# The down product of a mixture of experts turned: weights stationary, tokens moving

## What is computed

```python
gate = softmax(x @ Wg + bg); thr = sigmoid(x @ Wt + bt) * 0.125
adapted = gate - thr; w = adapted * (adapted >= 0)
w = w / where(sum(w) == 0, 1, sum(w))
h = gelu(einsum('td,edf->etf', x, W1) + b1[:, None, :])
eo = einsum('etf,efd->etd', h, W2) + b2[:, None, :]
out = einsum('te,etd->td', w, eo)
x = x + gb * out
```

## Time and profile before

| | |
|---|---|
| median of 3 runs | 1946.36 us (1943.92 to 1947.73) |
| the profiled execution, its own time | 1949.09 us |
| span of its trace | 1947.3 us |
| PE busy | 1807.6 us, 93%, 11616 matmuls |
| weight loads (PEld) | 1627.2 us, 84% |
| DVE, ACT, POOL busy | 1304.9 us (67%), 1048.1 us (54%), 756.0 us (39%) |
| DMA | 56.04 MB, 56434 packets |

### The profile page before, as it was taken

How to read it: one execution, slowest core, us unless ns; L and a number is a source line. 1 busy time by engine, 2 the same in 40 slices (tenths; PEclk the granted TensorE clock), 3 DMA queues, 4 the chain that set the end, 5 groups by cost and what they waited for, 6 DMA issues and landing times.

```text
span 1947.3 us, 32671 instructions
## 1 busy us (share of the span) xinstructions
PE 1807.6 (93%) x11616; PEld 1627.2 (84%) x11616; DVE 1304.9 (67%) x2472; ACT 1048.1 (54%) x2072; POOL 756.0 (39%) x1163
## 2 busy tenths in 40 slices
PE   5789947899589999999999999999999999999997
PEld 4679845798578999999999998888999999999996
DVE  3778747787666666666666666768666666666666
ACT  2567634676454555555555555554555555555553
POOL 4332124333364351615335161739244260624403
PEclk7999968999899999999999999999999999999998
DMA  4000000000000100101010010112110010101002
GB/s 112 26 15 23 18 11 17 23 18 9 31 23 23 33 23 22 42 4 44 11 34 31 14 44 1 33 33 89 53 33 22 23 34 12 44 12 33 12 1 65
DMA packets 56434, 56.04 MB, mean 29 GB/s; under 512 B 8384, under 2 KB 54480, under 8 KB 56272
## 3 DMA queue, kind: packets, MB, share of 16 engines
q1 hardware_dynamic: 56272, 53.95, 9.1%
HBM read 45.55 MB, written 8.39 MB: 28 GB/s over the span
## 4 chain that ended last, share of the span: by engine, by line
PE 62%; issue 5%; DVE 2%; ACT 2%; POOL 1%; POOLq 0%; DVEq 0%; ACTq 0%
PE score_ps L1075 10%; PE score_ps L1076 10%; PE score_ps L1077 9%; PE tr_ps L1110 5%; PE tr_ps L1108 5%; PE tr_ps L1106 5%; PE m_ps L1110 3%; PE m_ps L1108 3%; PE m_ps L1106 3%; PE o_ps L1108 3%; PE o_ps L1110 3%; PE o_ps L1106 3%; DVE h_lo L1276 1%; ACT h_hi L1209 1%; POOL h2f L1437 0%
## 5 line engine op out<-in xcount | busy, mean ns | idle before, releaser
L1205 ACT ACTIVATE g_sb<-c_sb,b_cols 128x512 f32<-128x512 f32 x384 | 276.0, 719 | 439.3 <-DVE c_sb L1340 288.1
L1276 DVE TENSOR_TENSOR h_lo<-g_sb,h_hi 128x512 fp32r<-128x512 f32 x512 | 398.6, 800 | 105.0 <-ACT h_hi L1209 105.0
L1075 PE MATMUL score_ps<-t_hi,w_hi 128*128 128x512 f32 x896 | 361.3, 403 | 27.6 <-ACT p_u L1235 12.2
L1076 PE MATMUL score_ps<-t_lo,w_hi 128*128 128x512 f32 x896 | 355.8, 397 | 0.0
L1077 PE MATMUL score_ps<-t_hi,w_lo 128*128 128x512 f32 x896 | 350.8, 392 | 0.0
L326 POOL TENSOR_TENSOR w_sums<-w_raw 128x128 f32<-128x128 f32 x64 | 42.7, 667 | 664.1 <-PE m_ps L1110 663.3
L1108 PE MATMUL tr_ps<-w_both,h_hi 128*128 128x256 f32 x1024 | 290.6, 284 | 0.0
L1110 PE MATMUL tr_ps<-w_both,h_lo 128*128 128x256 f32 x1024 | 290.5, 284 | 0.0
L1106 PE MATMUL tr_ps<-w_both,h_hi 128*128 128x256 f32 x1024 | 289.3, 283 | 0.0
L1209 ACT ACTIVATE h_hi<-c_sb,b_cols 128x512 fp32r<-128x512 f32 x384 | 271.6, 707 | 0.0
L1075 PEld LDWEIGHTS score_ps<-t_hi,w_hi 128*128 128x128 f32 x896 | 170.9, 191 | 54.5 <-ACT p_u L1235 12.2
(11 more groups left out here) (191 smaller groups left out, 4377.5 us busy)
## 6 DMA issues: line engine op xcount, KB each, us to landing
w_raw<-w_dram SPq DMA_DIRECT2D x128, 256.0 KB, 3.2
x_sb<-x_dram SPq DMA_DIRECT2D x32, 128.0 KB, 2.3
x_scratch<-x_sb SPq DMA_DIRECT2D x32, 128.0 KB, 1.7
t_sums<-x_scratch SPq DMA_DIRECT2D x8, 512.0 KB, 4.6
out_dram<-h2f SPq DMA_DIRECT2D x7, 512.0 KB, 3.2
probs_even<-wmod_dram SPq DMA_DIRECT2D x4, 256.0 KB, 3.9
probs_even<-wmod_dram SPq DMA_DIRECT2D x4, 128.0 KB, 2.3
probs_odd<-wqkvT_dram SPq DMA_DIRECT2D x1, 512.0 KB, 5.8
```

Source lines behind the costliest of these rows:

```text
L1075: nc.tensor.matmul(bank, hi, t_hi[p][:, b_, :], start=start, stop=False, skip_group_check=True)
L1076: nc.tensor.matmul(bank, hi, t_lo[p][:, b_, :], start=False, stop=False, skip_group_check=True)
L1205: nc.scalar.activation(g_sb[:, m % 2, :], source, ACT.Gelu_apprx_tanh, bias=bias).then_inc(act_g, 1)
L1276: nc.vector.tensor_tensor(h_lo[:, m % 6, :], g_sb[:, m % 2, :], h_hi[:, m % 6, :].bitcast(F32), ALU.subtract).then_inc(dve_lo, 1)
```

## The change

The down product is turned: the stationary operand is a block of 128 hidden by 128 model columns of W2, high or low part, and all 512 tokens of a unit of hidden values move. Its result is [model columns, tokens], one bank for each of two blocks of model columns and each unit. So the gate of a token now lies along the free dimension and has to be the same on all partitions: the gates are written to DRAM transposed, element by element, on SP at the end of each batch of attention, and a row of 1024 tokens is loaded for each round to all partitions (g_rows). b2 lies on partitions and is added in the eviction. The eviction is one DVE instruction per bank, `(y + b2) * g`, four per round; for expert 0 it writes the accumulator, for the others y_sb, which POOL adds to the accumulator. At the end the accumulator is transposed back by PE through bank_b (16 turns, each in a group of its own: 72 to 79 and 121 to 128, and four more at the very end), scaled by the output gate on DVE and added to x1 on POOL. The bias product is gone. Weight slots go from five to four, the hidden ring from six to five. The casts of the next pair's tokens move on ACT from the end of a group to behind p_u; the low parts of the token sums go from POOL to DVE.

```diff
-SLOTS = 5
+SLOTS = 4
+RING = 5
...
+gT_dram = nc.dram_tensor("gates_scratch", [B, E, T], F32).ap()
...
+                    for half in range(NT // GT):
+                        sp.wait_ge(*done(dve_G2, b, "G2", half, 0, G2_STEPS))
+                        for t in range(half * GT, (half + 1) * GT):
+                            sp.dma_start(gT_dram[b, :, t * P:(t + 1) * P].rearrange("e p -> p e"),
+                                         gates[:, b * NT + t, :], allow_slow_non_contiguous=True).then_inc(s_gT[b], 16)
...
+                    sp.dma_start(b2_cols[:], b2.rearrange("e (k p) -> p e k", p=P), allow_slow_non_contiguous=True).then_inc(l_b2, 16)
...
+                    def load_gates(r):
+                        b, e, p = parts(r * FS)[0:3]
+                        if e == 0 and p == 0:
+                            sp.wait_ge(s_gT[b], NT * 16)
+                        if r > 0:
+                            sp.wait_ge(dve_evict, r * 4)
+                        sp.dma_start(g_rows[:], gT_dram[b, e, p * 2 * UTOK:(p + 1) * 2 * UTOK].partition_broadcast(
+                            P)).then_inc(l_g, 16)
...
 def down(n, name):
-                        for j in range(UNIT):
-                            tok = slice(j * P, (j + 1) * P)
-                            nc.tensor.matmul(y_of(u, j), h_hi[:, ring, tok], w2_both[slot][:, f, 0, :], ...)
-                            nc.tensor.matmul(y_of(u, j), h_hi[:, ring, tok], w2_both[slot][:, f, 1, :], ...)
-                            nc.tensor.matmul(y_of(u, j), h_lo[:, ring, tok], w2_both[slot][:, f, 0, :], ...)
+                        for k in range(KD):
+                            if first and before >= 0:
+                                pe.wait_ge(dve_evict, before * 4 + u * 2 + k + 1)
+                            w_hi, w_lo = (w2_both[slot][:, f, i, k * P:(k + 1) * P] for i in range(2))
+                            o = y_banks[u][k]
+                            nc.tensor.matmul(o, w_hi, h_hi[:, ring, :], ...)
+                            nc.tensor.matmul(o, w_lo, h_hi[:, ring, :], ...)
+                            nc.tensor.matmul(o, w_hi, h_lo[:, ring, :], ...)
...
 def evict(n, u):      (DVE, in place of add)
+                        dve.wait_ge(l_g, (r + 1) * 16)
+                        to = acc_of(b, p, u) if e == 0 else y_sb[:, u, :, :]
+                        for k in range(KD):
+                            nc.vector.scalar_tensor_tensor(to[:, k, :], y_banks[u][k], b2_cols[:, e, k:k + 1],
+                                                           g_rows[:, u * UTOK:(u + 1) * UTOK], ALU.add,
+                                                           ALU.mult).then_inc(dve_evict, 1)
...
 def add(r):           (POOL)
+                        for u in range(2):
+                            pool.wait_ge(dve_evict, r * 4 + u * 2 + 2)
+                            nc.gpsimd.tensor_tensor(acc, acc, y_sb[:, u, :, :], ALU.add).then_inc(pool_acc, 1)
...
 def turned(...):      (PE)
+                        for i, t in enumerate(tiles):
+                            for k in range(KD):
+                                last = nc.tensor.transpose(bank[:, i * D + k * P:i * D + (k + 1) * P],
+                                                           source[:, k, t * P:(t + 1) * P], ident_sb[:])
+                        last.then_inc(made_by, 1)
...
 ACT loop
                         nc.scalar.activation(p1_u3[:], bank_a, ACT.Copy).then_inc(act_p1, 1)
+                        cast_tokens(n)
                         act.wait_ge(pe_prod, 7 * n + 3)
                         hidden(n, "c11", bank_a)
...
 DVE, before its loop
+                    dve.wait_ge(l_b2, 16)
```

More of the change, by code:

```diff
@@ new lines, in down, with turned, turn @@
+                        done_.then_inc(pe_down, 1)
+                    def turned(source, bank, tiles, made_by):
+                        for i, t in enumerate(tiles):
[3 more added lines that the diff above has]
+                        last.then_inc(made_by, 1)
+                    def turn(n):
+                        k = TURN_AT[n]
+                        b, p, u, half, r = turn_source(k)
+                        pe.wait_ge(dve_u2, min(n + 1, GROUPS))
+                        pe.wait_ge(pool_acc, adds_before(r, u) + 1)
+                        turned(acc_of(b, p, u), bank_b, (2 * half, 2 * half + 1), pe_turn)
@@ L1183, in _ @@
                             product(n, bank_h, S4, B22, False, True)
+                        else:
+                            pe.wait_ge(dve_evict, LAST * 4 + 2)
+                            for i, bank in enumerate((bank_a, bank_g)):
+                                if i == 0:
+                                    pe.wait_ge(act_hi, made(GROUPS - 1, "c11") + 1)
+                                else:
+                                    pe.wait_ge(dve_c21, GROUPS)
+                                turned(y_sb[:, 0, :, :], bank, (2 * i, 2 * i + 1), pe_fin)
                         if n > 0:
                             down(n - 1, "c12")
+                    pe.wait_ge(dve_evict, LAST * 4 + 4)
+                    pe.wait_ge(dve_c12, GROUPS)
+                    turned(y_sb[:, 1, :, :], bank_h, (0, 1), pe_fin)
+                    pe.wait_ge(dve_turn, len(TURNS))
+                    turned(y_sb[:, 1, :, :], bank_b, (2, 3), pe_fin)
                 @block.scalar
@@ L1248, in _ @@
                         hidden(n, "c12", c_sb[:, 0, :])
-                        cast_tokens(n)
                 @block.vector
@@ L1376, in _ @@
-                    nc.vector.tensor_tensor(half, half, slabs[1][:, 0:2, :], ALU.add).then_inc(dve_out, 1)
+                    turn(GROUPS)
+                    dve.wait_ge(dve_c22, GROUPS)
+                    dve.wait_ge(dve_c12, GROUPS)
+                    for i, (to, bank) in enumerate(((p1_u3[:], bank_a), (u2[:], bank_g))):
+                        dve.wait_ge(pe_fin, i + 1)
+                        scaled(to, bank, B - 1, dve_fin)
+                    evict(GROUPS - 1, 1)
+                    dve.wait_ge(dve_lo, 4 * GROUPS)
@@ new lines, in _ @@
+                    for i, (to, bank) in enumerate(((g_sb[:, 0, :], bank_h), (g_sb[:, 1, :], bank_b))):
+                        dve.wait_ge(pe_fin, i + 3)
+                        scaled(to, bank, B - 1, dve_fin)
+                    dve.wait_ge(dve_fin, 4)
+                    dve.wait_ge(pool_out, len(TURNS))
+                    tile = slabs[3].rearrange("p t d -> p (t d)")[:, 2 * D:4 * D]
+                    nc.vector.tensor_tensor(tile, tile, g_sb[:, 1, :], ALU.add).then_inc(dve_out, 1)
```

348 lines of the change are left out of this document (163 added, 185 removed).

## The result

The changed kernel takes 2068.5 us (median of 4 runs, 2060.0 to 2079.2), the kernel before 1947.1 beside it: ratio 1.063, 95% interval 1.058 to 1.068. The range ended at 1980. The profiled execution took 2060.0 us.

A forecast was written before the change was run, and what follows sets the result against it. TensorE's order of matmuls was taken to set the mixture's time. Terms -21 - 17 - 12 - 8 + 15 + 35 + 8 - 2 gave -2 us, 1944 from the median 1946.4, range 1918 to 1980.

The forecast's parts named there:

- Gate rows through DRAM: 32 element-wise gate DMAs on SP: batch 0's hide, batch 1's delay the mixture's start; +8 us, bounds +2 and +41.
- Down product: 48 matmuls of 256 columns become 24 of 512 per group: -21 us, bounds 0 and -23.
- Bias, token preparation: Bias work leaves expert 0's 16 groups, -17 us; token casts, sums and low parts move to waiting places, -12.
- Old finish, turning back: POOL's old work finishing both batches goes, -8 us; twenty turns of four transposes each come, +15, bounds +9 and +20.
- Sums on GpSimd: Two 1024-element POOL additions in 27 rounds hold up DVE's h_lo: +35 us, bounds 25 to 51, from below about 5.
- Tail: Work behind the last matmul gets some 2 us shorter: -2 us, bounds -4 and +1.
- Rival C: Element-wise DMA delays the mixture's start; at 3.2 us per gate DMA +34, 1978 us; chance 0.13.
- Rival E: The turned down product saves little or nothing, something else sets the step: +13 to +21, 1957 to 1965 us; chance 0.07.
- the walk: One round followed with a 2.4 us POOL addition behind each half's eviction: 1.3 us lost per round, 27 rounds, +35.
- Rival B: POOL's additions cost little, 0.3 us a round, 8 instead of 35, gate rows 3: 1912 to 1930 us; chance 0.26.
- D: Rival: the port is worse, additions at 2.8 us, two stalls, 2.5 us per round: +32, 1976 us; chance 0.12.

The follow-up runs named there:

- e1: The kernel before plus only the 32 gate DMAs in 4-byte pieces to DRAM, which nothing reads: 2100.7 us, ratio 1.080 to the kernel before.
- e5: e3 with each GpSimd sum cut to 16 elements per partition, leaving most expert results out of the output: 1871.3 us, ratio 0.959 to the kernel before.
- e3: The changed kernel with gates and b2 turned on TensorE instead of moved element by element: 1905.7 us, ratio 0.979 to the kernel before.
- e9: The kernel before plus only batch 0's sixteen gate DMAs in 4-byte pieces, which nothing reads: 2005.6 us, ratio 1.029 to the kernel before.
- e2: The changed kernel with gates turned on TensorE, b2 still loaded element by element: 1907.1 us, ratio 0.980 to the kernel before.
- e4: e3 with each down matmul in two halves of 256 tokens, same weights stationary: 1939.3 us, ratio 0.996 to the kernel before.
- e6: e3 with each GpSimd sum in four instructions of 128 x 256: 1869.5 us, ratio 0.959 to the kernel before.

## Where the prediction was right and where it failed

| term | predicted | measured | from |
|---|---|---|---|
| Gate rows through DRAM | +8 (+2 to +41) | +153.6 | e1 |
| Down product | -21 | -50 | 127 x (10.20 - 10.59) |
| Bias, token preparation | -29 | -31.1 | groups 0-8, 60-72: before against e5 |
| Old finish, turning back | +7 | +2.6 | groups 72-80, 120-127: before against e5 |
| Sums on GpSimd | +35 | +34.9 | e3 against e5 |
| Tail | -2 | -1.4 | last p_u to the span's end, before and after |

The rows sum to +109, against +110.9 in the profiled execution and +121.4 between the medians (the changed kernel's runs spread from 2060 to 2079); the rest is not attributed.

**The step that failed is "Gate rows through DRAM".** It failed twice. The first error is "Nearest are the 256-byte pieces", 1.2 us per DMA. Those were loads of SBUF; the gates are written to DRAM in pieces of 4 bytes, and one DMA takes 5.7 us in place of 1.2. Even the upper bound, 3.2 us from the mean of the run, was short: it too averaged packets that are mostly something else, and no row of before had small pieces going to DRAM. The second error is that batch 0's "hide", since "SP's next work waits until 311.20". That holds only below (311.20 - 263.45) / 16 = 3.0 us per DMA, and the text's own upper price of 3.2 broke it. The bound was put on batch 1 alone; the same price had to be put on both. With 5.7 us each, batch 0 costs 58.5 (e9) and batch 1 about 95 (153.6 - 58.5). Of these 84 stand ahead of the first p_u (it comes at 678.15 in e1 and at 594.37 in e9), at the barrier, where the loss was named but sized at 5 us.

Rival C had the right mechanism and the sign, "element-wise DMA delays the start of the mixture", and a price of +34 because it took over those two errors. Its condition, the first p_u after 550, came true (675.66). But it put element-wise DMAs under one price, and b2's, which are loads, cost nothing (e2).

**The down product** was mis-sized, -21 against -50 measured (its own product, 24 x 0.0065 x 128, is 20). The step of a down matmul was taken as 0.232, that of the up products in the same trace; it is 0.2267, and the up products, counted as unchanged, fell to the same. The 512-column step of before was itself longer because it stood among 256-column steps, which e4 shows by bringing it back. -50 lies beyond both bounds, since they moved the down's steps alone. Rival E is out. The rule of the Trainium skill, "TensorE: Matmul & The Clock Gate", that was weighed there (the page gives it for the isolated gap) would have given -8. The trace disagrees with it by about 0.010 us at either width: 0.119 against 0.109 at 256 columns, 0.2267 against 0.216 at 512. So there is a surplus for each matmul, and 24 matmuls fewer in a group make the down's gain 0.27 us instead of 0.06; the rest of the 50 is the up products'.

**The sums** came out as walked: 1.67 us are lost in a round of the first pair and 0.63 in one of the second, mean 1.15 where 1.3 was walked; 27 of them are 31, and the rest of the 34.9 stands in groups 60 to 80 and the last ones, where token preparation and turns add to it. The bounds beside the walk had the wrong measure: they went by POOL's total time, which e6 raises at no cost. What Rival B had against itself, that the splits' pieces last 0.7 us and not 2.4, is the point that decided. So Rivals B and D fall. h_lo's mean rose to 0.97 as expected. Bias, token preparation and tail stand within some 2 us. The turns cost 9.0 us in e5's groups 72 to 80 and 120 to 127, where 15 was taken for all twenty, and the old finish was 6.4 in the same groups, where 8 was taken. RING and SLOTS were not tried alone; with them as changed, 8 to 60 holds no extra in e5 and e6, so they cost nothing there.

Had the gate rows been free, the other terms would have given 1936 and the kernel takes 1906. So the sum was 30 us off in its other terms, nearly all of it the down product, and 145 us off in the one that had no row near it.

## What to carry to other kernels

Ask of every new DMA how many pieces it has, how long each is and which way it goes: 4-byte pieces written transposed into DRAM cost about 0.09 us each on one of 16 engines, hold the issuing queue for as long, and so everything queued behind, while 32-byte pieces written there as they lay and 4-byte pieces read held up nothing. Write such data in longer pieces, or turn it on TensorE first (here two transposes and two DMAs took the place of a 150 us delay). When a price is bounded from both sides, put the upper bound into every sentence that says "hides". When GpSimd and VectorE both work in SBUF, cut GpSimd's instructions short: in pieces of 256 columns, sums that had cost 35 us cost nothing.

## What was unexpected of the hardware

- A DMA of 1024 pieces of 4 bytes takes 5.7 us of the queue when it writes to DRAM, and an issue of 0.68 us is all that shows when it reads from DRAM into SBUF.
- In DRAM writes a piece of 32 bytes, as the gates lie, costs under 58 ns per engine (8.5 in the packets' records), one of 4 bytes in the transposed order 93; there a tenth of the packets hold nine tenths of the time.
- A 512-column matmul step is 0.2267 us in a stream of its like and 0.233 behind 256-column steps (0.119 each), which is worth 0.12 us of a group's 10.6.
- POOL work in shorter instructions takes longer itself (198 against 136 us for the same sums) and yet frees VectorE, in steps: 49.2, 19.0 and 14.3 us over plain groups with 1024, 512 and 256 columns.
